# Second attention: the value product moves between the two score slots of a step

## The reference

```
Q = x @ W_k.T                       # 16 heads, dk = 8
scores = -(|q|^2 - 2 q.t + |t|^2) / sqrt(dk)
attn = softmax(scores)              # over 1024 tokens, no mask
context = attn @ Q
out = (context @ merged / sqrt(dk)) @ W_o.T
```

## Time and profile before

| | |
|---|---|
| median of 3 runs | 1101.64 us (1101.56 to 1103.21) |
| profiled execution, its own time | 1099.16 us |
| its span, first to last instruction | 1097.4 us |
| TensorE matmul busy | 1004.7 us (92%) |
| ScalarE busy | 707.4 us (64%) |
| VectorE busy | 700.0 us (64%) |
| exponentials of the second attention (L1063) | 256, from 591.6 to 845.4 us, 238.7 us busy |
| mean granted TensorE clock | 0.961 |

### The profile page before, as it was taken

One profiled execution on the slowest core, in us unless ns is written; L12 is line 12 of the kernel. 1 busy time (PEld: TensorE's weight loads), 2 busy tenths in 40 slices (PEclk: granted clock), 3 DMA queues, 4 the chain that ended last, 5 costly groups with the idle time before them and its releaser, 6 DMA issues.

```text
span 1097.4 us, 18772 instructions
## 1 busy us (share of the span) xinstructions
PE 1004.7 (92%) x6927; PEld 596.8 (54%) x6927; DVE 700.0 (64%) x1454; ACT 707.4 (64%) x1031; POOL 556.2 (51%) x482
## 2 busy tenths in 40 slices
PE   4789999999999999999467999999998399999997
PEld 3456666666666666665353222233222277888786
DVE  6777777777777767773463223353122589999998
ACT  3356656666666656665224999999998376666564
POOL 2267877777787778778100000000000157887885
PEclk9899999999999999999768999999999689999999
DMA  2000000000000001100000000000000003121211
GB/s 94 8 9 9 8 9 1 9 8 9 8 9 8 8 8 19 40 1 1 1 1 3 9 12 13 10 9 13 13 8 9 4 1 118 58 94 60 77 39 39
DMA packets 24927, 23.52 MB, mean 21 GB/s; under 512 B 17612, under 2 KB 20316, under 8 KB 23820
## 3 DMA queue, kind: packets, MB, share of 16 engines
q1 hardware_dynamic: 24844, 22.42, 7.2%
HBM read 19.20 MB, written 1.11 MB: 19 GB/s over the span
## 4 chain that ended last, share of the span: by engine, by line
PE 66%; DVE 18%; issue 9%; ACT 3%; SPq 1%; POOL 1%; DMA 1%; DVEq 0%; ACTq 0%; POOLq 0%
PE banks L470 11%; PE banks L1054 10%; PE banks L1042 7%; DVE big L1359 5%; PE banks L338 5%; PE banks L395 4%; PE banks L444 4%; PE banks L478 3%; PE banks L489 3%; PE banks L450 3%; PE banks L448 3%; PE banks L446 3%; PE banks L421 2%; ACT prob L570 2%; PE banks L994 2%
## 5 line engine op out<-in xcount | busy, mean ns | idle before, releaser
L773 POOL TENSOR_TENSOR pacc<-pacc,prob 128x1024 f32<-128x1024 f32 (+3 forms) x160 | 274.7, 1717 | 58.4 <-ACT prob L570 46.8
L1063 ACT ACTIVATE prob<-banks 128x1024 f32<-128x1024 f32 x256 | 238.7, 1099 | 21.4 <-PE banks L1042 21.4
L570 ACT ACTIVATE prob<-banks 128x1024 f32<-128x1024 f32 (+1 forms) x160 | 150.4, 941 | 132.3 <-PE banks L450 128.0
L1392 POOL TENSOR_TENSOR big<-prob,big 128x512 fp32r<-128x512 f32 x108 | 165.1, 1548 | 59.7 <-ACT big L1342 33.0
L470 PE MATMUL banks<-prob,v 128*64 128x512 f32 (+3 forms) x768 | 142.7, 493 | 0.6 <-DVE zz L697 0.3
L1348 ACT ACTIVATE prob<-banks,w 128x512 f32<-128x512 f32 x144 | 94.4, 685 | 71.5 <-PE banks L1310 71.3
L1008 POOL TENSOR_TENSOR wqkv<-wqkv 64x512 f32<-64x512 f32 x8 | 8.3, 1032 | 258.0 <-DVE wqkv L1004 258.0
L1054 PE MATMUL banks<-prob,v 128*32 128x512 f32 x1024 | 137.1, 608 | 0.8 <-DVE pacc L1071 0.3
L1042 PE MATMUL banks<-big 32*128 32x512 f32 x512 | 108.9, 512 | 6.7 <-DVE big L1029 5.8
L1330 PE MATMUL banks<-big 128*128 128x512 f32 x432 | 106.7, 393 | 4.4 <-POOL big L1392 4.4
L1042 PEld LDWEIGHTS banks<-big 32*128 32x128 f32 x512 | 46.1, 185 | 116.5 <-ACT prob L1063 81.0
(11 more groups left out here) (221 smaller groups left out, 1704.5 us busy)
## 6 DMA issues: line engine op xcount, KB each, us to landing
prob<-gate_rows SPq DMA_DIRECT2D x8, 1024.0 KB, 4.7
w<-in_experts SPq DMA_DIRECT2D x9, 514.0 KB, 3.6
wqkv<-in_wqkv SPq DMA_DIRECT2D x16, 193.0 KB, 2.4
x<-in_x SPq DMA_DIRECT2D x4, 256.0 KB, 4.0
zz<-pacc SPq DMA_DIRECT2D x64, 16.0 KB
wpr<-pacc SPq DMA_DIRECT2D x64, 16.0 KB
out<-x SPq DMA_DIRECT2D x4, 256.0 KB, 2.3
wpr<-in_wpr SPq DMA_DIRECT2D x1, 512.0 KB, 6.0
```

Of the source, the lines that this page charges most:

```text
L570: act.activation(pr[:, g % NRING, :, 0:wd], banks[:, 2 * (j % 2):2 * (j % 2) + 2, 0:wd], ACT.Exp, scale=SCALE0).then_inc(s_exp, 1)
L773: pool.tensor_tensor(pacc[:, half, :, o:BLK], pacc[:, half, :, o:BLK], p_[:, :, at:at + wd], ALU.add).then_inc(s_padd, 1)
L1063: act.activation(prob[:, n % NP1, :], banks[:, 2 * (n % 3):2 * (n % 3) + 2, :].rearrange("p b c -> p (b c)"), ACT.Exp, scale=2 * SCALE1).t ...
L1392: pool.tensor_tensor(act2[1][:, tb % 2, i, :], hid[:, tb % 2, i, :], act2[0][:, tb % 2, i, :], ALU.subtract).then_inc(s_hlP, 1)
```

## The change

In each step the value product of the step two back is issued between the two score slots instead of behind them. The extras of a step stay behind everything else of it, so they now stand directly behind the odd score slot.

```
@@ -1111,10 +1111,10 @@
             for u in range(NB1):
                 for i in range(2 * TB):
                     scores1_pe(pe, u, 2 * i)
-                    scores1_pe(pe, u, 2 * i + 1)
                     m = 2 * TB * u + i
                     if m >= 2:
                         pv1_pe(pe, m - 2)
+                    scores1_pe(pe, u, 2 * i + 1)
                     if u == GROUPS and i in (0, 12):
                         out1_pe(pe, 0, i // 12, 7)
                     if u == NB1 - 1 and i == 2 * TB - 1:
```

## The result

The changed kernel takes 1106.99 us in the median of 16 runs, the kernel before beside it 1102.05 us; the ratio is 1.0036 (95% interval 1.0023 to 1.0049), so about 4.0 us slower (2.5 to 5.4); the two medians differ by 4.9. A second measurement gave 1.0042 (1.0027 to 1.0058). The forecast was 1104.3 us, 2.7 us slower, in a range of 1101.0 to 1106.6: the direction was right, the size too small, and the median lies 0.4 us above the range. Against the measured 1102.05 of before, a larger sample than the three runs that the forecast started from, the change is 4 to 5 us where 2.7 was expected.

A forecast was written before the change was run, and what follows sets the result against it. ScalarE's exponentials bound the kernel, TensorE late only behind extras. Terms +2.0 (units 1, 2, 3, 5, 6), +0.7 (unit 0), +0.8 (unit 4), -0.9 (end), plus proj hundredths, gave +2.7 us: 1104.3 us, range 1101.0 to 1106.6.

The forecast's parts named there:

- ScalarE is the bound, TensorE is late only behind extras: Second attention: exponentials bind every step without an extra; the change can gain at most their stalls, 21.4 us idle.
- A lone slot costs as much as a pair, 0.43: Score slot issued without its partner, ahead of heads or proj: holds TensorE 0.43 us, as a pair does with 0.44.
- rival 2: Lone slots ahead of heads and proj are cheap, 0.22 us each: 1.7 us faster in all, 1099.9 us; chance 0.12.
- The stall moves to the next odd slot and doesn't shrink: Behind proj: next even slot in time, following odd slot stalls 0.44 us against 0.43 before.
- Rival 3: Stalls behind heads and proj go, as the odd slot behind is in time too: -9.5 us, 1092.1 us; chance 0.05.
- Units 1 to 6: Second attention: +0.4 us in each of units 1, 2, 3, 5, 6 (+2.0), and +0.8 in unit 4.
- The end, -0.9: Output DMA chain from unit 7's first half starts with a value product one slot earlier: 0.9 us gained.
- What a norm holds back: At norm: it holds back only the slot on its own rows; stall 0.44 us before and after, no change.
- Unit 0, +0.7: First unit, at half clock: exponential of slot 7 ends 0.45 us later; with steps 4 and 9, +0.7 us.
- Rival 1: Unit 0: earlier product fills TensorE's gap, clock rises earlier, -1.2 us; total +1.5, 1103.1 us; chance 0.17.

The follow-up runs named there:

- extras_inside: The changed kernel with heads, proj, norm and unit 4's output projections directly behind the value product, ahead of the odd slot; ratio 0.9966 against the kernel before.
- unit7_new: The kernel before, with the new order (value product between the two score slots) in unit 7 alone; ratio 0.9985 (0.9968 to 1.0001).

## Why the prediction was right, and where it was too small

- **ScalarE is the bound, TensorE is late only behind extras.** Right; unit 7 is 29.33 us under both orders.
- **A lone slot costs as much as a pair, 0.43.** Right at the place that no row of before showed (638.39 to 638.82), so rival 2 is out; extras_inside, which keeps the pairs, shows the same from the other side.
- **The stall moves to the next odd slot and doesn't shrink.** Right to within 0.02. Stalls of unit 1 in the changed kernel: 0.52, 0.16, 0.51, 0.46, 0.45, 0.45; the working gave 0.51, then 0.15 and 0.50, then 0.44 for each norm and the second proj. They stand ahead of exponentials 7, 10, 11, 13, 21 and 23, the places that the prediction names. Rival 3 is out.
- **Units 1 to 6.** +0.4 each and +0.8 in unit 4 forecast, +0.41 and +0.83 measured, the earlier chain ahead of unit 4 (stall 0.34 instead of 0.84, then 0.50) included.
- **The end, -0.9.** Right, and shown by the traces of unit7_new and of the changed kernel.
- **What a norm holds back.** The prediction lets it hold back only the slot on its own rows. In the changed kernel this makes no difference; extras_inside shows that the order of issue decides it too.
- **Unit 0, +0.7: the term that was mis-sized.** It measured +2.35. The working up to slot 6 held; it failed in taking the clock's rise from the trace of before, at the same distance from the start. The half clock lasted 3.41 us longer, and the product and the pair behind the heads ran in it: exponential 7 ended 1.64 later than before where 0.45 was reckoned, and from there to exponential 13, behind the proj of step 4, another 0.45 was lost beyond what was reckoned. Rival 1 had seen that the change can move the clock at this place, and had the sign wrong: I took a gap filled in TensorE's records for an earlier rise. With 2.35 for 0.7 the sum is 2.6 + 1.65 = 4.3, the 4.35 of the traces and within the interval of the ratio.

## What to carry to other kernels

When the bound engine is fed through a ring, work out the margin of a plain step and what each extra takes from it: here 0.62 us against about 1.0 for whole heads and 1.05 for a whole proj. The order of this change only moved the stalls. In these runs a stall went where the extra was no larger than what the steps ahead of it had left of the margin: cutting the extras in two and spreading them brought 6.3 us between the spans, the better order of extras_inside 3.1. Two slots on different rows took 0.44 us together and 0.43 us each when something of another kind stood between them: look at what an edit puts between such instructions, and at a stretch on the edge between two clocks don't assume that the clock will rise where it did.
